# Last adjacency pair in two loads, one cast and some row ends moved between engines, and a later read of the flag that guards a second pass

## Chip, cores and metric

The kernel runs on one core of a Trainium2 chip. The metric is the device time of one execution in microseconds: the median of three runs is 112.62 us, with a lowest of 112.59 and a highest of 112.67.

## What is computed

Eight graphs of 1024 nodes with 128 features each. `adj` holds 0 or 1 as int32, so of the four relations only the first can occur, and the weights of the others matter only in a second pass described below.

```python
# x: (8, 1024, 128) f32, adj: (8, 1024, 1024) int32, weight: (4, 128, 128), bias: (128,)
masks = (relation[None] == rel_ids[:, None, None, None]).astype(x.dtype)
h = einsum('rbnm,bmd->rbnd', masks, x)
y = einsum('rbnd,rdo->bno', h, weight) + bias
out = layernorm(x + y, axis=-1)        # eps 1e-5, no gain and no offset
```

The adjacency is 33.6 MB of the 37.8 MB that are read; 4.2 MB are written.

## The kernel before, in words

A *unit* is 128 rows of the adjacency of one batch (512 KB, `adj_sb[:, slot, u]`), a *pair* two of them (1 MB), a *group* four units, or fewer in the last batch, which is split into a (units 0, 1), a2 (2, 3), c (4, 5), e (6) and d (7). `LAST` is the index of group a. A *set* of rows is what is normalised and stored together: one for each of the batches 0 to 6 (the seventh is called `full`), and two for batch 7, `ra` (units 0 to 3) and `rb` (units 4 to 7).

Loads. SyncE's queue issues all adjacency loads in order, batch 0 a unit at a time and the others a pair at a time (L414), with the loads of x between them; a slot of `adj_sb` is filled again when the pair that lay in it three batches before has been read by ScalarE (L408). After the last load the same queue issues the nine stores (L417), each when its set is normalised.

ScalarE reads each pair once, in `check` (L548): it writes `bytes_of` (fp8, two units interleaved, so that one transpose carries both) and leaves in `squares` a sum that is too large if an entry is neither 0 nor 1. It also copies `h` out of PSUM (L568), casts x to fp16 for batches 0 and 1 (L561), masks the last two odd units (L597), takes roots (L573) and normalises some rows (L583).

TensorE transposes a pair (L667) or, in batch 0, a unit (L658), multiplies the masked unit by the high and low part of x (L689), and projects with the weight (L702). For the last two batches x times the weight (`z`) is formed at the start and the product is direct (`rows_of_unit`, L743). `idle_turns` (L759) are matmuls of zeros ahead of the first unit. In `step_by_two` (L793) the transpose of the next pair stands before the two products of the group; for the pairs 4 and 5 alone it stands between them (L799 to L803).

VectorE masks the transposed unit (L875), adds x (L885), takes statistics (L891, L897, L902), the first guess of the inverse root (L912, `offer_guess`), and for `rb` the whole root (L917 to L936) and the rows of e and d (L941). `find_far` and `find` (L953 to L967) reduce what was gathered about the inputs to `found`; TensorE sums it (L838), VectorE copies the sum to `again` (L1048), and every engine loads `again` into a register and branches over a second pass (L301) that does not run on these inputs.

GpSimd casts x to fp16 for the batches from 2 on (L453), forms the low part (L459), adds the bias (L465), refines the roots of all sets but `rb` (L484 to L501) and normalises most rows (L512).

The end, in the order of the programs. GpSimd: roots of `full`, units 0 to 3 of `full`, roots of `ra`, units 0 and 1 of `ra`, unit 4 of `rb`. ScalarE: masks of units 5 and 7, root of `ra`, units 4 to 7 of `full`, root of `rb`, units 2 and 3 of `ra`, unit 5 of `rb`. VectorE: the list in the diff's last hunk. A store of one of the last three sets waits for GpSimd (`s_norm`) and for ScalarE (`s_aside`); that of `rb` for VectorE too (`s_done`). SyncE then branches at L301 and waits for the stores to land (L295, L296), which ends the program.

Of the kernel before, what the change touches and what calls it, by code (L numbers as in the profile page):

```python
# [5 lines left out]
P = 128  # L6
# [15 lines left out]
SLOPE = 4.25 ** 0.5  # L22
# [28 lines left out]
def adj_resnorm_kernel(nc, x, adj, weight, bias, out):  # L51
# [91 lines left out]
    with ctx:  # L143
# [49 lines left out]
        squares = sb("squares", [P, B * PAIRS], FP32)  # L193
# [40 lines left out]
        s_adj = [[sem(f"adj_loaded{slot}{k}") for k in range(PAIRS)] for slot in range(ADJ_SLOTS)]  # L234
        s_out = sem("rows_stored")
# [162 lines left out]
        def _(sp):  # L398
# [24 lines left out]
            load_x(1)  # L423
            for b in range(EARLY, B):
                for k in range(PAIRS):
                    load_adj(b, k)
                    if k == PAIRS - 1 and b + 1 < B - 2:
                        load_x(b + 1)
# [12 lines left out]
        def _(pool):  # L441
# [7 lines left out]
            def split_hi(b):  # L449
                pool.wait_ge(s_x[b], 16)  # L450
                pool.wait_ge(s_prod, last_group_of(b - 2) + 1)
                pool.wait_ge(s_rm, b - 1)
                nc.gpsimd.tensor_copy(x_hi[:, b % 2], x_sb[:, b]).then_inc(s_hi, 1)  # L453
# [66 lines left out]
            for b in range(B - 1):  # L520
                if b + 1 < B - 2:
                    if b:
                        split_hi(b + 1)
                    split_lo(b + 1)
                    add_bias(b + 1)
                if b >= 1:
                    roots(sets[b - 1])
                    normalise(sets[b - 1], sets[b - 1].units)
            full, ra, rb = sets[B - 2:]
            roots(full)  # L530
            normalise(full, full.units[:4])
# [6 lines left out]
        def _(act):  # L538
            def check(b, k):
# [5 lines left out]
                else:  # L545
# [4 lines left out]
                                     accum_out=squares[:, at:at + 1]).then_inc(s_check, 1)  # L550

# [64 lines left out]
            for g in groups[1:LAST]:  # L616
# [4 lines left out]
                for n, at in enumerate(range(pairs_checked_by(groups[g.index - 1]), pairs_checked_by(g))):  # L621
# [3 lines left out]
                    if n == 0 and g.index == 1:  # L625

                        split_hi(1, slice(0, J), s_x[1], s_hi)
# [3 lines left out]
            check(e.b, e.first // 2)  # L631
# [4 lines left out]
            normalise(full, full.units[4:]).then_inc(s_aside, 1)  # L636
            root(rb)
            normalise(ra, ra.units[2:]).then_inc(s_aside, 1)
# [4 lines left out]
        def _(pe):  # L643
# [119 lines left out]
            idle_turns(20, 2)  # L763
# [29 lines left out]
            def step_by_two(g, units, b, k):  # L793
                if not packed(b, k):
# [3 lines left out]
                    products(g, units, x_lo)  # L798
                elif pair_no(b, k) < FIRST_PACKED + 2:  # L799

                    products(g, units, x_hi)
                    transpose_pair(b, k)
                    products(g, units, x_lo)  # L803
                else:
                    transpose_pair(b, k)
                    for part in (x_hi, x_lo):
                        products(g, units, part)
# [35 lines left out]
        def _(dve):  # L843
            s_odd, s_far, s_wrong = (sem(n) for n in ("odd_ready", "far_ready", "wrong_ready"))
            s_st = sem("stats_ready")
# [113 lines left out]
            def find():  # L959

                dve.wait_ge(s_check, B * PAIRS)
                nc.vector.tensor_reduce(odd[:, 2:3], squares[:, :], AX.X, ALU.max).then_inc(s_odd, 1)
                dve.wait_ge(s_odd, 3)
                nc.vector.tensor_scalar(wrong[:, :], odd[:, 2:3], 2.0 * N * MIDDLE + 4.0, None, ALU.is_gt).then_inc(s_wrong, 1)
                dve.wait_ge(s_far, 2)
# [27 lines left out]
            for g in groups[1:LAST]:  # L993
# [9 lines left out]
                if g.index == LAST - 1:  # L1003
# [24 lines left out]
            statistics(a)  # L1028
            mask_unit(e.b, e.first)
            sum_rows(a2)  # L1030
            offer_guess(r)
            statistics(a2)
            combine(ra, a2, ra.units)
            sum_rows(c)
            statistics(c)
            combine(rb, c, c.units)
            offer_guess(ra)
            statistics_of_sum(e)
            combine(rb, e, e.units)
            statistics_of_sum(d)  # L1040
            combine(rb, d, d.units)
            find()
# [4 lines left out]
            dve.wait_ge(s_count, 1)  # L1047
            nc.vector.tensor_copy(again[:, :], ids_t[1][0:1, 0, 0:2].bitcast(FP32)).then_inc(s_again, 1)  # L1048
# [18 lines left out]
```

## Time and profile before

| | |
|---|---|
| median of three runs | 112.62 us |
| the profiled execution | 112.82 us |
| its span | 110.9 us |
| mean granted TensorE clock | 0.978 |
| busy | PE 89%, DVE 77%, ACT 76%, POOL 63% |
| DMA over the span | 42.23 MB, mean 381 GB/s |

The profile shows one execution on the core. The span is the stretch from its first to its last instruction, and 1.9 us of the profiled time lie outside of it. PE is TensorE's matmul side, PEld its weight loads, DVE VectorE, ACT ScalarE, POOL GpSimd, SP SyncE; a trailing q marks an engine's queue, where it issues transfers, waits or branches. L548 is line 548 of the kernel. All times in rows are microseconds from the start of the span unless ns is written.

### The profile page before, as it was taken

What the parts mean: (1) busy time and instruction counts of PE and PEld (TensorE: products, weight loads), DVE (VectorE), ACT (ScalarE), POOL (GpSimd) and SP (SyncE); (2) the same over time, 40 slices, a digit from 0 to 9 for tenths busy, and PEclk for the clock granted to TensorE, in tenths of its full rate; (3) what the DMA queues carried; (4) which work ended last, traced back from release to release, by engine and by line L of the source; (5) the groups of instructions that cost most, each with busy time, mean ns of one, the idle gap of its engine ahead of it and who ended that gap; (6) DMA issues with size and microseconds to landing.
All of it is one profiled execution on the core that took longest, in us unless ns stands there. A gap on an engine that the chain in (4) does not pass through costs nothing.

```text
span 110.9 us, 3073 instructions
## 1 busy us (share of the span) xinstructions
PE 99.1 (89%) x1118; PEld 91.6 (83%) x1118; DVE 85.2 (77%) x254; ACT 84.5 (76%) x103; POOL 70.1 (63%) x135
## 2 busy tenths in 40 slices
PE   5969999998999999999999999999999999996000
PEld 4639999997898999999998999899999999996000
DVE  1034677548999999999999896989794999999600
ACT  0444758999969897979798978996979998778320
POOL 3000699006969899989998999895187049518720
PEclk9999999999999999999999999999999999999965
DMA  3999999999999999999999999999999999991450
GB/s 50 359 420 420 421 422 440 419 425 422 420 425 425 422 428 417 425 427 420 427 422 424 427 425 422 428 428 428 414 425 428 419 424 418 408 384 74 191 191 9
DMA packets 7794, 42.23 MB, mean 381 GB/s; under 512 B 865, under 2 KB 994, under 8 KB 4194
## 3 DMA queue, kind: packets, MB, share of 16 engines
q1 hardware_dynamic: 7344, 40.44, 88.1%
q10 hardware_dynamic: 434, 1.57, 3.6%
q8 instruction: 10, 0.16, 0.6%
q14 instruction: 6, 0.05, 0.1%
HBM read 37.81 MB, written 4.19 MB: 379 GB/s over the span
## 4 chain that ended last, share of the span: by engine, by line
PE 52%; DMA 27%; ACT 6%; POOL 5%; DVE 2%; issue 2%; SPq 1%; POOLq 0%; DVEq 0%
DMA adj_sb<-adj 27%; PE h_ps L689 19%; PE h_ps L743 8%; PE ids_t L667 8%; ACT bytes_of L548 6%; PE y_ps L702 5%; PE ids_t L658 4%; POOL x_sb L512 3%; DVE mask_t L875 2%; PE y_ps L743 2%; SPq L414 1%; PE spare L722 1%; PE h_ps L722 1%; PE y_ps L722 1%; PE other L722 1%
## 5 line engine op out<-in xcount | busy, mean ns | idle before, releaser
L548 ACT ACTIVATE bytes_of<-adj_sb,offset 128x2048 fp8e4<-128x2048 int32 x32 | 64.0, 2003 | 4.3 <-DMA adj_sb<-adj 3.8
L875 DVE TENSOR_SCALAR mask_t<-ids_t 128x1024 uint16<-128x1024 uint16 x62 | 40.0, 681 | 11.8 <-PE ids_t L658 10.9
L689 PE MATMUL h_ps<-mask_t,x_hi 128*128 128x256 bf16 (+1 forms) x200 | 25.5, 272 | 0.9 <-DVE mask_t L875 0.9
L689 PE MATMUL h_ps<-mask_t,x_lo 128*128 128x256 bf16 (+1 forms) x200 | 25.5, 272 | 0.0
L512 POOL TENSOR_SCALAR x_sb<-x_sb,rstd,shift 128x128 f32<-128x128 f32 x55 | 23.8, 449 | 0.9
L689 PEld LDWEIGHTS h_ps<-mask_t,x_hi 128*128 128x128 f16 x200 | 18.3, 100 | 3.5 <-DVE mask_t L875 1.7
L465 POOL TENSOR_TENSOR x_sb<-x_sb,bias_sb 128x1024 f32<-128x1024 f32 x6 | 14.3, 2380 | 10.7 <-ACT bias_sb L609 10.3
L689 PEld LDWEIGHTS h_ps<-mask_t,x_lo 128*128 128x128 f16 x200 | 19.3, 100 | 2.1
L667 PE MATMUL ids_t<-ident,bytes_of 128*128 128x128 bf16 x224 | 18.6, 226 | 0.1
L667 PEld LDWEIGHTS ids_t<-ident,bytes_of 128*128 128x128 bf16 x224 | 17.2, 148 | 0.7 <-ACT bytes_of L548 0.5
L459 POOL TENSOR_TENSOR x_lo<-x_sb,x_hi 128x1024 f16<-128x1024 f32 x5 | 10.7, 2143 | 7.2 <-ACT x_hi L561 6.9
L891 DVE BATCH_NORM_STATS2 stats<-x_sb 128x6 f32<-128x128 f32 x62 | 13.6, 280 | 0.0
L702 PE MATMUL y_ps<-w_sb,h_all 128*128 128x128 f32 x96 | 12.7, 276 | 0.0
L568 ACT ACTIVATE h_all<-h_ps 128x512 f32<-128x512 f32 x12 | 7.2, 597 | 6.2 <-PE h_ps L689 6.2
L702 PEld LDWEIGHTS y_ps<-w_sb,h_all 128*128 128x128 f32 x96 | 11.7, 192 | 0.1
L743 PE MATMUL h_ps<-z_hi,mask_t 128*128 128x128 f16 x96 | 11.4, 220 | 0.0
L743 PE MATMUL h_ps<-z_lo,mask_t 128*128 128x128 f16 x96 | 11.4, 220 | 0.0
L885 DVE TENSOR_TENSOR x_sb<-y_ps,x_sb 128x512 f32<-128x512 f32 (+1 forms) x13 | 8.6, 663 | 3.4 <-PE y_ps L702 3.3
L743 PEld LDWEIGHTS h_ps<-z_hi,mask_t 128*128 128x128 bf16 x96 | 9.4, 98 | 0.0
L743 PEld LDWEIGHTS h_ps<-z_lo,mask_t 128*128 128x128 bf16 x96 | 9.4, 98 | 0.0
L850 DVE TENSOR_REDUCE row_max<-x_hi 128x8 f32<-128x1024 f16 x6 | 7.3, 1210 | 0.0
L759 PE MATMUL h_ps<-mask_t 128*128 128x256 bf16 (+1 forms) x22 | 5.5, 430 | 1.2 <-DVE mask_t L970 1.2
(102 smaller groups left out, 107.8 us busy)
## 6 DMA issues: line engine op xcount, KB each, us to landing
adj_sb<-adj SPq DMA_DIRECT2D x28, 1024.0 KB, 24.6
adj_sb<-adj SPq DMA_DIRECT2D x8, 512.0 KB, 10.1
out<-x_sb SPq DMA_DIRECT2D x7, 512.0 KB, 21.3
x_sb<-x SPq DMA_DIRECT2D x5, 512.0 KB, 24.1
x_sb<-x ACTq DMA_DIRECT2D x3, 512.0 KB, 7.5
out<-x_sb SPq DMA_DIRECT2D x2, 256.0 KB, 3.2
w_sb<-weight SPq DMA_DIRECT2D x1, 64.0 KB, 6.0
bias_row<-bias ACTq DMA_DIRECT2D x1, 0.5 KB
```

What stands on the lines that cost most here:

```text
L459: nc.gpsimd.tensor_tensor(x_lo[:, b % 2], x_sb[:, b], x_hi[:, b % 2], ALU.subtract).then_inc(s_lo, 1)
L465: nc.gpsimd.tensor_tensor(x_sb[:, b], x_sb[:, b], bias_sb[:, :].unsqueeze(1).to_broadcast([P, J, D]), ALU.add).then_inc(s_xb, 1)
L512: last = nc.gpsimd.tensor_scalar(rows[:, slot, u, :], rows[:, slot, u, :], rstd[:, slot, u:u + 1], shift[:, slot, u:u + 1], ALU.mult, ALU.add)
L548: nc.scalar.activation(bytes_of[:, at % ROOM].rearrange("p n t -> p t n"), adj_sb[:, slot, 2 * k:2 * k + 2, :], ACT.Square, scale=SLOPE, b ...
L667: last = nc.tensor.transpose(bank[:, j, :], words[:, j // step(b), j % step(b), :], ident[:, :])
L689: last = nc.tensor.matmul(h_ps[g.bank][:, to], part[:, g.b % 2, j, :], mask_t[:, g.b % 2, j, cols], start=(j == 0 and part is x_hi), stop= ...
L702: last = nc.tensor.matmul(y_of(g)[:, n, :], h_all[:, g.bank, n * P:(n + 1) * P], w_sb[:, 0, :], start=True, stop=True)
L743: last = nc.tensor.matmul(y_of(g)[:, u - g.first, :], mask_t[:, g.b % 2, j, u * P:(u + 1) * P], part[:, g.b - (B - 2), j, :], start=(j == ...
L850: nc.vector.tensor_reduce(row_max[:, b, :], x_hi[:, b % 2], AX.X, ALU.max, apply_absolute_value=True).then_inc(s_rm, 1)
L875: nc.vector.tensor_scalar(mask_t[:, b % 2, :, u * P:(u + 1) * P].bitcast(UINT16), ids_t[bank_of(turn)][:, :, :].bitcast(UINT16), 1 << bit, ...
L885: nc.vector.tensor_tensor(rows[:, g.b, g.us, :], y_of(g)[:, 0:g.count, :], x_sb[:, g.b, g.us, :], ALU.add).then_inc(s_sum, 1)
L891: last = nc.vector.bn_stats(stats[:, u, :], rows[:, g.b, u, :])
```

## The change

- The last pair (batch 7, units 6 and 7) is loaded as two units with a semaphore each; ScalarE reads them one by one into the same place of `bytes_of`, and their two sums are joined by a new VectorE instruction.
- The high part of x for batch 1 is cast by GpSimd and no longer by ScalarE.
- The transposes of pairs 4 and 5 stand before both products, as the others do.
- `idle_turns` at the start are 44 of 128 columns where there were 20 of 256.
- `find_far` comes one group earlier. `find` is cut into four: join, largest, wrong, and the rest, which are spread over the last groups and stand ahead of the combination for e.
- `offer_guess` of `full` stands ahead of the mask of e.
- Units 2 and 3 of `full` pass from GpSimd to ScalarE, which does them after the root of `rb`; the signal that lets `full` be stored is now theirs.
- VectorE copies `again` only when all rows have been normalised by GpSimd and ScalarE.

```diff
-        squares = sb("squares", [P, B * PAIRS], FP32)
+        squares = sb("squares", [P, B * PAIRS + 1], FP32)
...
+            def load_last(u, signal):
+                free(B - 1, u // 2)
+                sp.dma_start(adj_sb[:, (B - 1) % ADJ_SLOTS, u:u + 1, :], rows_of(adj, B - 1, u, 1)).then_inc(signal, 16)
+
             for b in range(EARLY, B):
                 for k in range(PAIRS):
+                    if (b, k) == (B - 1, PAIRS - 1):
+                        load_last(J - 2, s_first)
+                        load_last(J - 1, s_second)
+                        continue
                     load_adj(b, k)
...
                 if b + 1 < B - 2:
-                    if b:
-                        split_hi(b + 1)
+                    split_hi(b + 1)
                     split_lo(b + 1)
...
             roots(full)
-            normalise(full, full.units[:4])
+            normalise(full, full.units[:2])
             roots(ra)
...
+            def check_last_pair():
+                at = B * PAIRS - 1
+                room(at)
+                for t, loaded in enumerate((s_first, s_second)):
+                    act.wait_ge(loaded, 16)
+                    last = nc.scalar.activation(bytes_of[:, at % ROOM, :, t], adj_sb[:, (B - 1) % ADJ_SLOTS, J - 2 + t, :],
+                                                ACT.Square, scale=SLOPE, bias=offset[:, 0:1], saturate=False,
+                                                accum_out=squares[:, at + t:at + t + 1])
+                last.then_inc(s_check, 1)
...
-                    if n == 0 and g.index == 1:
-
-                        split_hi(1, slice(0, J), s_x[1], s_hi)
...
-            check(e.b, e.first // 2)
+            check_last_pair()
             root(full)
             mask_second(c.units[1])
             mask_second(d.first)
             root(ra)
-            normalise(full, full.units[4:]).then_inc(s_aside, 1)
+            normalise(full, full.units[4:])
             root(rb)
+            normalise(full, full.units[2:4]).then_inc(s_aside, 1)
             normalise(ra, ra.units[2:]).then_inc(s_aside, 1)
...
-            idle_turns(20, 2)
+            idle_turns(44, 1)
...
-                elif pair_no(b, k) < FIRST_PACKED + 2:
-
-                    products(g, units, x_hi)
-                    transpose_pair(b, k)
-                    products(g, units, x_lo)
                 else:
...
+            def join_last_pair():
                 dve.wait_ge(s_check, B * PAIRS)
-                nc.vector.tensor_reduce(odd[:, 2:3], squares[:, :], AX.X, ALU.max).then_inc(s_odd, 1)
+                last = B * PAIRS - 1
+                nc.vector.tensor_tensor(squares[:, last:last + 1], squares[:, last:last + 1], squares[:, last + 1:last + 2],
+                                        ALU.add).then_inc(s_joined, 1)
+
+            def find_largest():
+                dve.wait_ge(s_joined, 1)
+                nc.vector.tensor_reduce(odd[:, 2:3], squares[:, 0:B * PAIRS], AX.X, ALU.max).then_inc(s_odd, 1)
...
-                if g.index == LAST - 1:
+                if g.index == LAST - 2:
                     find_far()
...
             statistics(a)
+            offer_guess(r)
             mask_unit(e.b, e.first)
+            join_last_pair()
             sum_rows(a2)
-            offer_guess(r)
+            find_largest()
             statistics(a2)
             combine(ra, a2, ra.units)
             sum_rows(c)
+            find_wrong()
             statistics(c)
             combine(rb, c, c.units)
             offer_guess(ra)
             statistics_of_sum(e)
+            find()
             combine(rb, e, e.units)
             statistics_of_sum(d)
             combine(rb, d, d.units)
-            find()
...
             dve.wait_ge(s_count, 1)
+
+            dve.wait_ge(s_norm, len(sets))
+            dve.wait_ge(s_aside, 3)
             nc.vector.tensor_copy(again[:, :], ids_t[1][0:1, 0, 0:2].bitcast(FP32)).then_inc(s_again, 1)
```

## Rows read from the trace of the kernel before

**Rows 1.** The page's 40 equal slices of the span: DMA engines' busy share, in tenths.
```profile
DMA  3999999999999999999999999999999999991450
```

**Rows 2.** The chain that ended last: start us, us, what.
```profile
44.68 24.71 DMA adj_sb<-adj
...
71.57 0.71 PE ids_t L667 x8
...
97.69 0.51 PE ids_t L667 x8
```

**Rows 3.** Timeline of the first 28 us: start, us, engine, line, instruction, count, [idle before].
```profile
1.19 4.45 PE L759 MATMUL h_ps<-mask_t 128*128 128x256 bf16 x20 [1.19 <-DVE mask_t L970]
...
24.91 1.07 ACT L561 ACTIVATE x_hi<-x_sb 128x1024 f16<-128x1024 f32 x1
...
27.89 1.05 PE L689 MATMUL h_ps<-mask_t,x_hi 128*128 128x256 bf16 x8 [0.51 <-DVE mask_t L875]
```

**Rows 4.** Timeline of ScalarE: its pass over the last pair.
```profile
93.88 2.01 ACT L548 ACTIVATE bytes_of<-adj_sb,offset 128x2048 fp8e4<-128x2048 int32 x1 [0.29 <-DMA adj_sb<-adj]
```

**Rows 5.** Timeline of VectorE, 98 to 105 us.
```profile
98.22 0.69 DVE L875 TENSOR_SCALAR mask_t<-ids_t 128x1024 uint16<-128x1024 uint16 x1 [0.21 <-PE ids_t L667]
...
99.16 0.20 DVE L912 RECIPROCAL first_guess<-std 128x8 f32<-128x8 f32 x1
...
101.57 0.18 DVE L902 BATCH_NORM_AGGREGATE moments<-stats 128x2 f32<-128x6 f32 x1
101.80 0.30 DVE L897 BATCH_NORM_STATS2 stats<-spare 128x6 f32<-128x128 f32 x1
102.13 0.18 DVE L902 BATCH_NORM_AGGREGATE moments<-stats 128x2 f32<-128x6 f32 x1
102.23 0.15 DVE L962 TENSOR_REDUCE odd<-squares 128x1 f32<-128x32 f32 x1
...
103.03 0.27 DVE L967 TENSOR_SCALAR found<-wrong,high,low 128x1 f32<-128x1 f32 x1 [0.46 <-DVE wrong L964]
...
104.73 0.13 DVE L1048 CAST again<-ids_t 1x1 int32<-1x1 f32 x1
```

**Rows 6.** Timeline of GpSimd and ScalarE, 99 to 106 us.
```profile
99.51 0.20 POOL L489 TENSOR_TENSOR product<-sixteenth,first_guess 128x8 f32<-128x8 f32 x1 [2.19 <-DVE first_guess L912]
...
100.99 1.74 POOL L512 TENSOR_SCALAR x_sb<-x_sb,rstd,shift 128x128 f32<-128x128 f32 x4
...
102.46 0.28 ACT L573 ACTIVATE std<-moments,eps 128x4 f32<-128x4 f32 x1
...
104.68 1.26 ACT L583 ACTIVATE x_sb<-x_sb,shift,rstd 128x128 f32<-128x128 f32 x3 [1.94 <-POOL shift L501]
104.76 1.31 POOL L512 TENSOR_SCALAR x_sb<-x_sb,rstd,shift 128x128 f32<-128x128 f32 x3
```

**Rows 7.** Timeline of SyncE's queue: the stores of `full` and of `rb`.
```profile
102.75 0.33 SPq L417 DMA_DIRECT2D out<-x_sb  x1
```
```profile
106.10 0.37 SPq L417 DMA_DIRECT2D out<-x_sb  x1
```

**Rows 8.** Stretches: length, PE, PEld, DVE, ACT, POOL busy (count), PEclk, DMA share, GB/s.
```profile
103.50:104.75 1.25, 0.05 (x2) 0.00 (x0) 1.15 (x7) 0.07 (x1) 0.83 (x4) 1.00 0.96 390
...
106.50:107.75 1.25, 0.00 (x0) 0.00 (x0) 0.00 (x0) 0.00 (x0) 0.00 (x0) 0.50 1.09 405
...
108.50:110.00 1.50, 0.00 (x0) 0.00 (x0) 0.00 (x0) 0.00 (x0) 0.00 (x0) 0.50 0.07 16
```

**Rows 9.** DMA begun in 107.4:107.7: packets, MB, share of 16 engines over 0.3 us.
```profile
q8 instruction: 1, 0.02, 28.7%
```

**Rows 10.** DMA issues from 106 us on: count, KB, us from issue to landing.
```profile
out<-x_sb SPq DMA_DIRECT2D x1, 256.0 KB, 4.3
```

**Rows 11.** Queue instructions of two lines: count, ns min/median/max, first and last start.
```profile
L301 PEldq COMPARE_BRANCH  x1: 453/453/453, 105.8 to 105.8; - x1
```
```profile
L296 SPq EVENT_SEMAPHORE  x1: 17/17/17, 110.4 to 110.4; - x1
```

More of the change, by code:

```diff
@@ L234, in adj_resnorm_kernel @@
         s_adj = [[sem(f"adj_loaded{slot}{k}") for k in range(PAIRS)] for slot in range(ADJ_SLOTS)]
+        s_first, s_second = sem("last_pair_first_unit_loaded"), sem("last_pair_second_unit_loaded")
         s_out = sem("rows_stored")
@@ L450, in split_hi @@
                 pool.wait_ge(s_x[b], 16)
-                pool.wait_ge(s_prod, last_group_of(b - 2) + 1)
-                pool.wait_ge(s_rm, b - 1)
+                if b >= 2:
+                    pool.wait_ge(s_prod, last_group_of(b - 2) + 1)
+                    pool.wait_ge(s_rm, b - 1)
                 nc.gpsimd.tensor_copy(x_hi[:, b % 2], x_sb[:, b]).then_inc(s_hi, 1)
@@ L844, in _ @@
             s_odd, s_far, s_wrong = (sem(n) for n in ("odd_ready", "far_ready", "wrong_ready"))
+            s_joined = sem("last_squares_joined")
             s_st = sem("stats_ready")
@@ L957, in find_far, with find_wrong, find @@
                 nc.vector.tensor_scalar(low[:, :], odd[:, 1:2], LEAST, None, ALU.is_lt).then_inc(s_far, 1)
-            def find():
+            def join_last_pair():
                 dve.wait_ge(s_check, B * PAIRS)
-                nc.vector.tensor_reduce(odd[:, 2:3], squares[:, :], AX.X, ALU.max).then_inc(s_odd, 1)
+                last = B * PAIRS - 1
[4 more added lines that the diff above has]
+                nc.vector.tensor_reduce(odd[:, 2:3], squares[:, 0:B * PAIRS], AX.X, ALU.max).then_inc(s_odd, 1)
+            def find_wrong():
                 dve.wait_ge(s_odd, 3)
                 nc.vector.tensor_scalar(wrong[:, :], odd[:, 2:3], 2.0 * N * MIDDLE + 4.0, None, ALU.is_gt).then_inc(s_wrong, 1)
+            def find():
                 dve.wait_ge(s_far, 2)
```

## The prediction

> **What bounds the kernel now.** I read the page's slices first, then the chain of work that ended last, then the timeline of every engine over the last 15 us, and last the DMA traffic after the final store. The slices show the DMA engines full from the second slice to the thirty-sixth [rows 1]: the loads never pause. The chain shows what that means for the front of the kernel. It goes back from TensorE's transposes at 71.57 through ScalarE's pass over a pair to a load that was issued at 44.68 and landed 24.71 us later, at 69.39 [rows 2]. So up to 71.57 the time is set by how fast bytes arrive, and TensorE, though almost always busy, is there only as early as the data. From 71.57 to the transposes of the last pair at 97.69 the chain is TensorE's own work in one piece [rows 2]. Then comes an end that belongs to the small engines and the stores: the last matmul is over about 101.75 (VectorE's statistics of the last unit start at 101.80 [rows 5]), the last store is issued at 106.10 [rows 7], lands 4.3 us later [rows 10], SyncE passes its last wait at 110.4 [rows 11], and the span ends at 110.9. Nine microseconds therefore lie behind the last product. That is where I look for an effect.
>
> **The front: idle turns, cast, transposes.** The 20 turns of 256 columns take 4.45 us, 0.22 each [rows 3]; 44 of 128 columns at half that pace take 4.9 and end near 6.1, still before or at the first unit, whose transposes start at 6.37 in the chain's time. The cast of 1.07 us leaves ScalarE at 24.91 [rows 3] and goes to GpSimd, which has a hole there. The moved transposes fill a stall of TensorE of 0.51 us at 27.89, where it waits for a mask [rows 3]; VectorE's own order is not changed there, so the mask itself comes at most 0.1 to 0.2 us sooner. Between 0 and 0.7 us is won at 28 us. What hides it is the load that lands at 69.39: TensorE would only wait longer at 71.57 [rows 2]. I cost all three at nothing, and keep 0.3 us of gain as the outer bound, in case a part passes the load.
>
> **The last pair in two loads.** ScalarE starts on the pair at 93.88, 0.29 us after it was free, and takes 2.01 [rows 4], so `bytes_of` is there at about 95.9; TensorE comes for it just before 97.69 [rows 2]. In two halves the first can start earlier and the second ends, at a 1024-column price of 1.07 each [rows 3], by 95.7 to 96.1. Gain and loss both lie under 1.6 us of cover. They would count only if the second unit landed more than 1.6 us late. Nothing.
>
> **VectorE's end.** `find_far` moves into a gap. The first guess of `full` is now taken before the mask at 98.22, ahead of which VectorE idles 0.21 us [rows 5], so at about 97.95 in place of 99.16: 1.2 us earlier. Against that, three small instructions (join, largest, wrong) and the last of `find` now come before the statistics of d. A small one costs about 0.10, the distance of 102.13 to 102.23 [rows 5]; `found` 0.2 to 0.3. Less the guess that left (0.12) this is 0.3 to 0.4 us, with only 0.05 of slack (101.57 + 0.18 against 101.80 [rows 5]). So the variances of `rb` come 0.3 later and its root on ScalarE at 102.8, not 102.46 [rows 6]. It is paid back at once: before, `found` stood in front of the inversion and began at 103.03 after 0.46 us of idling [rows 5], so the inversion started at 103.2; now nothing stands there and it starts at 103.1. At worst `found` idles 0.46 in its new place too, and everything of `rb` comes 0.4 later.
>
> **GpSimd and ScalarE.** GpSimd takes 1.48 us from the first product to the first row (99.51 to 100.99) and 0.43 a row [rows 6]. With the guess 1.2 earlier it starts on `full` at 99.8 and is through its two rows at 100.7, not 102.7. The roots of `ra` then wait for VectorE's guess of `ra`, which follows the combination of c and comes some 0.2 before the 101.57 of e's, so by 101.4, and give rows from 103.2 on, not 104.76 [rows 6]; GpSimd ends at 104.6. ScalarE does `full` 4 to 7 from 100.5 to 102.2, the root of `rb` at 102.8, and then five rows in one go. Three took 1.26, so 0.39 a row and 0.49 for the last [rows 6]: from 103.0, `full` is complete at 103.9, `ra` at 104.65, `rb` at 105.05. ScalarE is now last. The store of `full` is issued at 103.9, 1.15 later than the 102.75 of before; that of `rb` at 105.05, 1.05 earlier than 106.10 [rows 7].
>
> **The stores.** Bytes of `full` flow from 103.5, 0.8 us after its issue, for 1.3 us; those of `ra` and `rb`, together as many, from 106.5 for another 1.3 to 1.4 [rows 8]. Now they queue behind one another: 103.9 + 0.8 + 2.65 = 107.35, against 107.9. If only this counted, the gain would be 0.5 us, not 1.05.
>
> **The wait before `again`.** This is the step that decides. After 107.9 the DMA engines are almost still, yet SyncE waits to 110.4. What moves in between is a trickle of 16 GB/s, some 24 KB between 108.5 and 110.0 [rows 8]: packets of the last store on one engine. That engine had been given something else. At about 107.5 a packet of the instruction queue begins, 16 KB, with 28.7% of 16 engines times 0.3 us, that is 1.38 us on a single engine [rows 9]. I take it to be caused by the branch over the second pass: `again` is there at 104.86 [rows 5], TensorE's branch runs at 105.8 and takes 453 ns [rows 11], and the fetch begins 2.65 us after `again`. Before, it fell into the middle of the last store's bytes. Now VectorE holds `again` for ScalarE's last row. Queued behind that wait are only the copy and VectorE's own branch; who waits for the copy is the branch of each engine, SyncE's among them, and that comes after the stores are issued and needs 1 us, long before they land. `again` comes at 105.05 + 0.1 to 0.5 (the 0.46 of `found` is the nearest row for a VectorE instruction after a late second wait) + 0.13 = 105.3 to 105.7, and the fetch at 107.9 to 108.3, when the bytes have been gone since 107.35. The last store then lands, like before, 0.5 us after its last byte (110.4 against 109.9), at 107.85, and the span ends 0.5 us after that (110.9 against 110.4), at 108.4.
>
> The Trainium skill has a rule on this (Runtime: NRT & Kernel Launch, Instruction fetch mechanics): engines stream their instructions in blocks of 16 KiB through DMA, which is "mostly hidden", and a taken branch to a place outside the window forces a fetch before the engine goes on. The size agrees with the packet in the row; "mostly hidden" does not, since here the fetch seems to hold up a store. By the word hidden the wait would be worth nothing.
>
> **The sum.** Span 110.9 to 108.4, less 2.5 us. Of the profiled 112.82 that leaves 110.3; the median lies 0.2 below the profiled execution, so 112.62 - 2.5 = 110.1. I add 0.1 for the worse end of `found`: 110.2.
>
> **Rivals.**
> 1. *A part of the collision stays* (0.20). A smaller instruction fetch falls among the 2.65 us of queued bytes, or the fetches come earlier than reckoned. It costs the engine 0.5 to 1.4 us of the 2.5: 110.7 to 111.6. For it: the queue of bytes is now longer. Against it: 0.55 us of margin.
> 2. *The fetch is not the cause* (0.11): the trickle belongs to an engine that is behind anyway. Then only the stores' 0.5 us remain, 112.1. Against it: the trickle follows right on the fetch [rows 8, 9].
> 3. *Slower* (0.10). `full` is stored 1.15 later, and the bytes of all three sets end late on the one engine. If they end after 107.9, the fetch still meets them, but starts later than before: what followed its start at 107.5 took 2.9 us to the landing, so 107.9 to 108.3 + 2.9 = 110.8 to 111.2, a span of 111.3 to 111.7 and 113.0 to 113.4 us. It decides from 0.55 us of lateness on.
> 4. *The front's gain passes the loads* (0.06), on top of my forecast: 109.9. Rows 2 speak against it.
> 5. *Gains and losses of the end cancel* (0.03), at 112.6.
>
> **How the numbers follow.** My forecast has 0.50, at 109.9 to 110.6 by the bounds of `found` and of the copy. With rivals 1, 2 and 4 the chance of faster is 0.87, of no change 0.03, of slower 0.10. About 0.2% is what a measurement of this kernel can tell from no change. The range goes from 109.8 to 112.1, which leaves out rivals 3 and 5 and some of the edges.
>
> **What would show it.** Right: the idle of 0.51 at 28 us gone and a longer wait for ScalarE or the load near 71; TensorE's last transposes still near 97.7; `full` stored near 103.9 and `rb` near 105.1; the copy of `again` after 105.1; the 16 KB instruction packet after the last store's bytes; a landing of 2.8 us in place of 4.3. Wrong: the last transposes earlier than 97.4 (then the loads didn't hold the front), or a last landing still over 4 us.

## The result and the profile after

The changed kernel takes 109.77 us (median of four runs, 109.71 to 109.82), where the one before takes 112.65 beside it. The ratio is 0.974, with a 95% interval of 0.9722 to 0.9757: 2.9 us less. The forecast was 110.2, with a range that began at 109.8. So the direction holds and the mechanism of the wait too, the gain was put 0.4 us too small, and the time lies 0.03 us below the range of 109.8 to 112.1. The profiled execution has a span of 107.9 us.

The chain that ended last, after (start us, us, what; the load's number of L414 is L416 here, L667 is L686):

```profile
44.71 24.71 DMA adj_sb<-adj
...
71.60 0.71 PE ids_t L686 x8
...
97.72 0.51 PE ids_t L686 x8
```

These are [rows 2] moved by 0.03 us. The front of the kernel has changed and everything from the load at 44.71 on stands where it stood. Nothing of the front's changes is to be seen at 71.60. ScalarE's pass over the last pair (timeline of ScalarE) comes in two parts of 1.14 us, at 93.52 and 94.65, that end at 95.8, 1.9 us before TensorE wants them. The second is:

```profile
94.65 1.14 ACT L568 ACTIVATE bytes_of<-adj_sb,offset 128x1024 fp8e4<-128x1024 int32 x1
```

All of the gain is made behind 97.6 us. First VectorE's timeline there, the answer to [rows 5]:

```profile
97.64 0.19 DVE L927 RECIPROCAL first_guess<-std 128x8 f32<-128x8 f32 x1
98.25 0.69 DVE L890 TENSOR_SCALAR mask_t<-ids_t 128x1024 uint16<-128x1024 uint16 x1 [0.43 <-PE ids_t L686]
98.86 0.15 DVE L978 TENSOR_TENSOR squares<-squares 128x1 f32<-128x1 f32 x1
...
99.38 0.49 DVE L906 BATCH_NORM_STATS2 stats<-x_sb 128x6 f32<-128x128 f32 x2
...
100.20 0.39 DVE L900 TENSOR_TENSOR x_sb<-h_ps,x_sb 128x256 f32<-128x256 f32 x1
100.50 0.14 DVE L987 TENSOR_SCALAR wrong<-odd 128x1 f32<-128x1 f32 x1
100.62 0.49 DVE L906 BATCH_NORM_STATS2 stats<-x_sb 128x6 f32<-128x128 f32 x2
...
101.37 0.27 DVE L912 BATCH_NORM_STATS2 stats<-other 128x6 f32<-128x128 f32 x1
101.55 0.26 DVE L992 TENSOR_SCALAR found<-wrong,high,low 128x1 f32<-128x1 f32 x1
101.73 0.17 DVE L917 BATCH_NORM_AGGREGATE moments<-stats 128x2 f32<-128x6 f32 x1
101.83 0.30 DVE L912 BATCH_NORM_STATS2 stats<-spare 128x6 f32<-128x128 f32 x1
102.16 0.18 DVE L917 BATCH_NORM_AGGREGATE moments<-stats 128x2 f32<-128x6 f32 x1
102.71 0.18 DVE L932 RECIPROCAL last_guess<-std 128x4 f32<-128x4 f32 x1 [0.36 <-ACT std L594]
...
104.73 0.15 DVE L1079 CAST again<-ids_t 1x1 int32<-1x1 f32 x1 [0.35 <-ACT x_sb L604]
```

The guess of `full` is at 97.64 in place of 99.16. The last combination, at 102.16, is 0.03 us later than before, although join, largest, wrong and found now stand ahead of it. The inversion starts at 102.71; before, it had to let `found` pass and started at 103.2. Two more rows of before, the statistics of a2 and of e, are compared with 99.38 and 101.37 further down:

```profile
99.28 0.49 DVE L891 BATCH_NORM_STATS2 stats<-x_sb 128x6 f32<-128x128 f32 x2
...
101.27 0.27 DVE L897 BATCH_NORM_STATS2 stats<-other 128x6 f32<-128x128 f32 x1
```

GpSimd and ScalarE (their timelines, the answer to [rows 6]):

```profile
97.98 0.20 POOL L500 TENSOR_TENSOR product<-sixteenth,first_guess 128x8 f32<-128x8 f32 x1 [0.94 <-DVE first_guess L927]
...
99.47 0.89 POOL L523 TENSOR_SCALAR x_sb<-x_sb,rstd,shift 128x128 f32<-128x128 f32 x2
...
103.07 1.33 POOL L523 TENSOR_SCALAR x_sb<-x_sb,rstd,shift 128x128 f32<-128x128 f32 x3
```
```profile
102.58 2.02 ACT L604 ACTIVATE x_sb<-x_sb,shift,rstd 128x128 f32<-128x128 f32 x5
```

The last row is ready at 104.60 on ScalarE, and at 106.07 before. The stores follow (SyncE's timeline, then the window 106 to 107 and the one behind it, with the columns of [rows 8]):

```profile
103.52 1.10 SPq L419 DMA_DIRECT2D out<-x_sb  x2
104.72 0.40 SPq L419 DMA_DIRECT2D out<-x_sb  x1
```
```profile
106.00:107.00 1.00, 0.00 (x0) 0.00 (x0) 0.00 (x0) 0.00 (x0) 0.00 (x0) 0.50 0.97 371
107.00:107.50 0.50, 0.00 (x0) 0.00 (x0) 0.00 (x0) 0.00 (x0) 0.00 (x0) 0.50 0.07 16
```

The bytes of all three sets flow without a gap until 107.0 and stop; no trickle follows. The instruction packets come after them. This is the DMA traffic of the window 107.3 to 107.7, in 40 slices of 0.01 us, where the only two slices with bytes are the starts of an 8 KB packet at 107.46 and of a 16 KB one at 107.63:

```profile
GB/s 0 0 0 0 0 0 0 0 0 0 0 0 0 0 0 0 819 0 0 0 0 0 0 0 0 0 0 0 0 0 0 0 0 1638 0 0 0 0 0 0
...
q8 instruction: 1, 0.02, 17.6%
```

SyncE passes its last wait at 107.4, before: 110.4 [rows 11] (the wait's line, L298 here):

```profile
L298 SPq EVENT_SEMAPHORE  x1: 17/17/17, 107.4 to 107.4; - x1
```

### The profile page after: what moved, and what is told of

Read it like the earlier page. It is cut to its first block, busy times and chain, and to the rows that moved or that the text cites. A ratio compares the mean times of both kernels' runs of the same rounds, so it can differ in the third digit from the quotient of the medians.

```text
span 107.9 us, 3126 instructions
## 1 busy us (share of the span) xinstructions
PE 99.2 (92%) x1142; PEld 92.2 (85%) x1142; DVE 85.0 (79%) x255; ACT 85.4 (79%) x106; POOL 70.5 (65%) x134
## 4 chain that ended last, share of the span: by engine, by line
DMA 45%; PE 25%; SPq 16%; ACT 6%; DVE 3%; issue 2%; DVEq 0%
DMA adj_sb<-adj 45%; SPq L416 10%; PE h_ps L762 8%; PE h_ps L708 6%; PE ids_t L686 5%; ACT bytes_of L558 4%; SPq L405 3%; PE y_ps L721 3%; ACT x_sb L604 2%; PE y_ps L762 2%; SPq L402 1%; DVE stats L906 1%; DVE moments L917 1%; DVE x_sb L900 1%; SPq L394 0%
## 5 line engine op out<-in xcount | busy, mean ns | idle before, releaser
L558 ACT ACTIVATE bytes_of<-adj_sb,offset 128x2048 fp8e4<-128x2048 int32 x31 | 62.1, 2003 | 5.9 <-DMA adj_sb<-adj 5.3
L523 POOL TENSOR_SCALAR x_sb<-x_sb,rstd,shift 128x128 f32<-128x128 f32 x53 | 23.1, 456 | 0.9
L686 PE MATMUL ids_t<-ident,bytes_of 128*128 128x128 bf16 x224 | 19.0, 228 | 0.5 <-ACT bytes_of L558 0.5
L686 PEld LDWEIGHTS ids_t<-ident,bytes_of 128*128 128x128 bf16 x224 | 16.9, 148 | 2.4 <-ACT bytes_of L558 2.1
L721 PE MATMUL y_ps<-w_sb,h_all 128*128 128x128 f32 x96 | 12.7, 276 | 0.0
L470 POOL TENSOR_TENSOR x_lo<-x_sb,x_hi 128x1024 f16<-128x1024 f32 x5 | 10.7, 2140 | 0.4
L464 POOL CAST x_hi<-x_sb 128x1024 f16<-128x1024 f32 x5 | 5.2, 1047 | 6.7 <-DMA x_sb<-x 6.7
```

What stands on the lines that cost most here:

```text
L470: nc.gpsimd.tensor_tensor(x_lo[:, b % 2], x_sb[:, b], x_hi[:, b % 2], ALU.subtract).then_inc(s_lo, 1)
L523: last = nc.gpsimd.tensor_scalar(rows[:, slot, u, :], rows[:, slot, u, :], rstd[:, slot, u:u + 1], shift[:, slot, u:u + 1], ALU.mult, ALU.add)
L558: nc.scalar.activation(bytes_of[:, at % ROOM].rearrange("p n t -> p t n"), adj_sb[:, slot, 2 * k:2 * k + 2, :], ACT.Square, scale=SLOPE, b ...
L686: last = nc.tensor.transpose(bank[:, j, :], words[:, j // step(b), j % step(b), :], ident[:, :])
L721: last = nc.tensor.matmul(y_of(g)[:, n, :], h_all[:, g.bank, n * P:(n + 1) * P], w_sb[:, 0, :], start=True, stop=True)
```

## Experiments

The moment at which TensorE is done with the last pair shifts from execution to execution by a few tenths, with the landing of the load that holds the front. So beside each span stands the start of VectorE's mask for unit 6 (the row with `mask_t<-ids_t` at 98.25 above), which follows TensorE's last transposes at once, and the *end*, the span less that start. It is the end that the changes behind 97.6 us act on. Span, mask and end are those of one profiled execution of each kernel; the medians are of 4 executions (9 for `a_early`), and each ratio is to executions of the kernel before that ran beside them, with medians of 112.41 us (`a_early` to `a_nofront`), 112.44 (`a_rows4`, `a_find_late`) and 112.61 (the last four). Spans are given to 0.1.

| kernel | median us | ratio to before, 95% interval | span | mask of unit 6 | end |
|---|---|---|---|---|---|
| before | 112.65 | | 110.9 | 98.22 | 12.7 |
| changed | 109.77 | 0.974 (0.9722 to 0.9757) | 107.9 | 98.25 | 9.7 |
| a_early | 111.81 | 0.9937 (0.9907 to 0.9967) | 110.2 | 98.62 | 11.6 |
| a_nowait | 109.91 | 0.9769 (0.9719 to 0.9819) | 108.1 | 98.40 | 9.7 |
| b_wait | 110.90 | 0.988 (0.98 to 0.9959) | 109.0 | 98.37 | 10.6 |
| a_nofront | 109.56 | 0.9743 (0.9695 to 0.9792) | 107.6 | 97.92 | 9.7 |
| a_rows4 | 109.02 | 0.9686 (0.9654 to 0.9717) | 107.2 | 98.11 | 9.1 |
| a_find_late | 109.89 | 0.9773 (0.9743 to 0.9802) | 107.9 | 98.20 | 9.7 |
| r4_guess_late | 110.76 | 0.9837 (0.9796 to 0.9877) | 109.1 | 98.39 | 10.7 |
| r4_find_late | 109.37 | 0.9703 (0.9658 to 0.9749) | 107.7 | 98.52 | 9.2 |
| r4_oneload | 109.09 | 0.9709 (0.9664 to 0.9753) | 107.2 | 98.10 | 9.1 |
| r4_nowait | 109.12 | 0.9696 (0.9658 to 0.9734) | 107.3 | 98.24 | 9.1 |

### Does the flag's fetch hold up the stores?

The theory says that the copy of `again` sets off a 16 KB instruction fetch some 2.6 us later, which costs if bytes of the last store are still queued on its DMA engine. The rival says that the trickle of [rows 8] belongs to an engine that is slow anyway. `b_wait` adds only the wait to the kernel before:

```diff
             dve.wait_ge(s_count, 1)
+            dve.wait_ge(s_norm, len(sets))
+            dve.wait_ge(s_aside, 3)
             nc.vector.tensor_copy(again[:, :], ...)
```

> The kernel before, with nothing but the two waits ahead of the flag's copy. Theory of the fetch: the copy comes at 106.2 to 106.5, the 16 KB fetch at 108.9, a microsecond after the last bytes (107.9); the last store lands at 108.4, the span ends at 108.9 and not 110.9, time 110.6. So the wait alone would be worth 2.0 of the 2.9 us. Rival (slow engine): span 110.9 or slightly more, since the branches come later; time 112.6.

Measured: span 109.0, end 10.6 for 12.7, median 110.90 where the kernel before beside it has 112.41. The copy is at 106.31, the bytes are through by 108.0, and SyncE's wait is over at 108.5 (rows of the windows and of the wait's line, L296; the two instruction packets start at 108.7 to 108.9):

```profile
107.00:108.00 1.00, 0.00 (x0) 0.00 (x0) 0.00 (x0) 0.00 (x0) 0.00 (x0) 0.50 0.99 381
108.00:108.60 0.60, 0.00 (x0) 0.00 (x0) 0.00 (x0) 0.00 (x0) 0.00 (x0) 0.50 0.02 3
```
```profile
L296 SPq EVENT_SEMAPHORE  x1: 17/17/17, 108.5 to 108.5; - x1
```

The rows are stored at the same moments as before, counted from the mask of unit 6, and the trickle is gone. A wait that makes the flag 1.6 us later ends the kernel 2.1 us earlier by the two profiled executions. By the medians it is 1.5 us, and the interval of the ratio reaches from 0.5 to 2.2 us.

A part of the difference, and what the trickle is, can be read from the DMA traffic of the kernel before, in 40 slices of the windows 107.4:107.7 and 108.7:110.3:

```profile
GB/s 1092 273 546 0 0 273 273 546 0 546 1092 546 819 0 0 1 2458 546 273 273 546 1365 273 546 0 0 0 273 819 0 546 546 1092 273 546 0 0 273 273 546
```
```profile
GB/s 0 0 0 0 51 0 0 0 0 0 51 0 0 0 0 51 0 0 0 51 0 51 0 51 0 51 0 51 0 0 0 0 0 0 0 0 0 0 0 0
```

The 16 KB packet starts in the slice with 2458, at 107.52, and with the 1.38 us of [rows 9] it ends at 108.90; the first packet of the trickle starts in the slice from 108.86 to 108.90. So the trickle is what the engine with the fetch had left to do. The 1 just ahead of the fetch is the packet of 4 bytes with which an engine closes its part of a transfer, here of the store of `ra`. The other fifteen of them lie in 107.1 to 107.3. The engine was therefore about 0.2 us behind when the fetch came, and the rival has this much of the trickle on its side; why it was behind is open. `a_early` goes the other way in the changed kernel:

```diff
+            dve.wait_ge(s_count, 1)
+            nc.vector.tensor_copy(again[:, :], ...).then_inc(s_again, 1)
             for part in (invert, times_guess, times_guess_again, better_guess, shift_last):
...
-            dve.wait_ge(s_count, 1)
-            dve.wait_ge(s_norm, len(sets))
-            dve.wait_ge(s_aside, 3)
-            nc.vector.tensor_copy(again[:, :], ...).then_inc(s_again, 1)
```

> The changed kernel, but VectorE copies the flag right after the combination for d, without waiting for any row. Theory (the instruction fetches that follow the flag hold up the last stores): the 16 KB fetch follows the copy by 2.6 to 2.8 us, so it begins at 105.0 to 105.3, in the middle of the bytes of the last three stores (104.2 to 107.05 in the changed kernel). It costs their engine 1.1 to 1.7 us: span 109.0 to 109.7 instead of 107.9, time 110.9 to 111.5. Rival (the trickle at the end belongs to a slow engine, the flag has no part in it): span 107.9, or less because the last branches are over sooner; time 109.7 to 109.8.

Measured: span 110.2, end 11.6 for 9.7. The fetch lies where it was expected, in the window 104.80 to 104.95, among the bytes, and 62.3% of 16 engines times 0.15 us is 1.5 us of one engine (rows: that packet; the store of `rb`; all nine stores' issues, with their shortest, median and longest time in ns; the end of SyncE's last wait):

```profile
q8 instruction: 1, 0.02, 62.3%
```
```profile
105.09 1.58 SPq L419 DMA_DIRECT2D out<-x_sb  x1
```
```profile
L419 SPq DMA_DIRECT2D out<-x_sb x9: 332/1584/2106, 73.3 to 105.1; - x9
```
```profile
L298 SPq EVENT_SEMAPHORE  x1: 17/17/17, 109.6 to 109.6; - x1
```

The loss of 1.9 us is above the 1.1 to 1.7 that I gave it. The second row offers a reason: the issue of the last store takes 1.58 us in place of 0.40, and ends at 106.67, 0.3 us after the fetch. That the fetch holds it is argued and not shown, since the four issues of stores from 73 to 80 us, under the full traffic of the loads, take 2.10 us each in this run as in the changed kernel.

The two runs move nothing but the flag. The trickle goes when the flag is later and comes back when it is earlier (in `a_early` one engine still moves bytes at 109.19, the others are done by 107.96), which an engine that is slow by itself would not do. They don't part TensorE's 16 KB packet from whatever else follows the flag; but of the two instruction packets that come behind the flag it is the only one that starts before the other engines' last bytes, in the kernel before and in `a_early` alike; the one of 8 KB starts at 108.56 and 108.65, when they are done. From the start of the copy to that of this packet it is 2.2 to 2.9 us over these runs (102.63 to 104.87, 104.73 to 107.63). `a_nowait` takes the waits alone away and leaves the copy behind the rows of d:

```diff
             dve.wait_ge(s_count, 1)
-            dve.wait_ge(s_norm, len(sets))
-            dve.wait_ge(s_aside, 3)
             nc.vector.tensor_copy(again[:, :], ...)
```

> The changed kernel without the two waits ahead of the flag's copy; the copy still stands after the rows of d, so it comes at about 104.3 and not 104.73. Theory of the fetch: its start moves from 107.5 to about 107.0, just at the end of the last bytes at 107.04: between nothing and 1.4 us, span 107.9 to 109.3, most likely 108.2. Rival: 107.9 exactly, as the bytes end at the same time. With the early copy beside it this gives the dose: the farther ahead of the last bytes the flag comes, the longer the end.

Measured: end 9.7, as with the waits. The copy is at 104.44, and in the window 107.0 to 107.4 the trace has the last bytes and the start of the 16 KB packet (19.5% of 16 engines times 0.4 us, 1.25 us):

```profile
q8 instruction: 1, 0.02, 19.5%
```

It is a near miss: the last closing packet is at 107.19, and the fetch begins at 107.21. So in the changed kernel the waits are an insurance and not the gain itself. What moved the bytes ahead of the fetch there is that the rows are done 1.5 us earlier, while the copy, without its waits, would be only about 0.5 us earlier than before, counted from the mask of unit 6 (104.44 with the mask at 98.40, for 104.73 with the mask at 98.22). In the kernel before, the waits alone do it.

### Does the front count?

`a_nofront` puts the front of before into the changed kernel:

```diff
-            idle_turns(44, 1)
+            idle_turns(20, 2)
...
+                elif pair_no(b, k) < FIRST_PACKED + 2:
+                    products(g, units, x_hi)
+                    transpose_pair(b, k)
+                    products(g, units, x_lo)
...
-                    split_hi(b + 1)
+                    if b:
+                        split_hi(b + 1)
...
+                    if n == 0 and g.index == 1:
+                        split_hi(1, slice(0, J), s_x[1], s_hi)
```

> The changed kernel with the front as before: 20 idle turns of 256 columns, the transposes of pairs 4 and 5 between the products, the cast for batch 1 on ScalarE. Theory (the load that lands at 69.4 holds the front): transposes after it at 71.6 and the last ones at 97.7 as in both kernels, span 107.9 within 0.1, time 109.8. Rival (a part of the gain is the front's): 0.3 to 0.7 us longer, 110.1 to 110.5.

Measured: ratio 0.9743, the same as with the new front, and the same end. That the gain is absorbed by the loads, and not by VectorE, was to be shown by two kernels (one execution each) that load half as much from batch 3 on. Their output isn't the reference's, since half of each row is left over from an earlier batch.

```diff
+                cols = slice(0, N // 2 if b >= ADJ_SLOTS else N)
-                sp.dma_start(units_of(adj_sb[:, slot], b, 2 * k, 2), rows_of(adj, b, 2 * k, 2)).then_inc(s_adj[slot][k], 16)
+                sp.dma_start(units_of(adj_sb[:, slot], b, 2 * k, 2)[:, :, cols],
+                             rows_of(adj, b, 2 * k, 2)[:, :, cols]).then_inc(s_adj[slot][k], 16)
```

> The changed kernel, but from batch 3 on only the first half of each row of the adjacency is loaded (the last pair excepted); the rest is what an earlier batch left there, so 10 MB less come in and the output differs. Theory (the loads absorb the front's gain): no wait for a load between 45 and 94 us; with the loads out of the way TensorE's lead at 35 us is kept to the end, so that the last transposes come 0.4 to 0.9 us earlier than in the same kernel with the old front, its twin in this call.

> The twin: the old front (idle turns, transposes, cast) with the same halved loads from batch 3 on. Theory: last transposes 0.4 to 0.9 us later than with the new front. Rival (VectorE, which has hardly a gap between 28 and 58 us, gives the pace and takes the gain): no difference over 0.2 us, and the loads need not be named.

The pair gives the rival's answer. Its two executions differ by 0.07 us at 35 us, and by 0.07 at 72 us and at the end; the expected 0.4 to 0.9 was wrong. VectorE's masks near 35 and near 72 us, in the order before, changed, h_front, h_nofront:

```profile
35.23 1.25 DVE L875 TENSOR_SCALAR mask_t<-ids_t 128x1024 uint16<-128x1024 uint16 x2
...
72.32 0.69 DVE L875 TENSOR_SCALAR mask_t<-ids_t 128x1024 uint16<-128x1024 uint16 x1 [0.34 <-PE ids_t L667]
```
```profile
34.33 1.26 DVE L890 TENSOR_SCALAR mask_t<-ids_t 128x1024 uint16<-128x1024 uint16 x2
...
72.34 0.69 DVE L890 TENSOR_SCALAR mask_t<-ids_t 128x1024 uint16<-128x1024 uint16 x1 [0.35 <-PE ids_t L686]
```
```profile
35.13 1.26 DVE L891 TENSOR_SCALAR mask_t<-ids_t 128x1024 uint16<-128x1024 uint16 x2
...
71.76 1.29 DVE L891 TENSOR_SCALAR mask_t<-ids_t 128x1024 uint16<-128x1024 uint16 x2
```
```profile
35.20 1.26 DVE L899 TENSOR_SCALAR mask_t<-ids_t 128x1024 uint16<-128x1024 uint16 x2
...
71.83 1.29 DVE L899 TENSOR_SCALAR mask_t<-ids_t 128x1024 uint16<-128x1024 uint16 x2
```

With half the bytes the way from the first to the second takes 36.63 us in both. With all of them it takes 37.09 before and 38.01 in the changed kernel, which is 0.90 us ahead of the kernel before at 35 and level at 72. So the loads do take back a lead, and VectorE, which can do this way in 36.63, does not.

But the lead of 0.90 us is not the front's. Two more kernels with the old front and all loads have the same mask at 34.55 (`b_wait`) and 34.42 (`a_nofront`); the nine with the new front and all loads have it at 34.33 to 34.74. It is the profiled execution of before, at 35.23, that is late. The row of `a_nofront`, and VectorE in the 7 us before, in the changed kernel (the columns of [rows 8]):

```profile
34.42 1.26 DVE L898 TENSOR_SCALAR mask_t<-ids_t 128x1024 uint16<-128x1024 uint16 x2
```
```profile
28.00:35.00 7.00, 7.00 (x74) 6.49 (x72) 6.97 (x21) 5.86 (x6) 3.51 (x3) 1.00 1.02 430
```

TensorE's stall of 0.51 us near 28 us is gone with the new front (in `a_nofront` it is there, at 27.10), and nothing of it is left at 35. VectorE is busy for 6.97 of the 7 us between, 6.96 before, which fits the rival: it gives the pace there. That it is the cause is not shown. What these executions show is no gain above 0.1 us at 35 us, so the loads had nothing of the front to hide.

### What are the moves at the end worth?

`a_rows4` gives `full` its four rows on GpSimd back:

```diff
-            normalise(full, full.units[:2])
+            normalise(full, full.units[:4])
...
-            normalise(full, full.units[4:])
+            normalise(full, full.units[4:]).then_inc(s_aside, 1)
             root(rb)
-            normalise(full, full.units[2:4]).then_inc(s_aside, 1)
```

> The changed kernel with one part undone: GpSimd normalises units 0 to 3 of the set of batch 6 again, ScalarE units 4 to 7 only, so this set may be stored at about 102.2 and not 103.5. Theory (the 1 MB of the last three sets queues on the DMA engines and ends 2.7 us after the first bytes, whatever row is last): the first half is gone before the second begins, the last rows are ready at 104.6 to 104.7 as before, the last bytes go at 106.1 and not 107.05, span 107.0, time 108.8 to 109.0. Rival (the last row sets the end): span 107.9 to 108.1, since GpSimd has two rows more and the roots of the next set come 0.1 to 0.2 later.

Measured: 109.02 us, end 9.1 for 9.7. This version is faster than both kernels. GpSimd has time for the two rows while it waits for the guess of `ra` (idle 0.65 us there in the changed kernel). The store of `full` is issued at 102.08, 1.4 us earlier, and its bytes are gone before the others begin (SyncE's timeline and the windows):

```profile
102.08 0.33 SPq L419 DMA_DIRECT2D out<-x_sb  x1
...
104.04 0.81 SPq L419 DMA_DIRECT2D out<-x_sb  x2
```
```profile
104.25:104.75 0.50, 0.00 (x0) 0.00 (x0) 0.14 (x1) 0.05 (x1) 0.19 (x1) 0.81 0.00 0
104.75:106.25 1.50, 0.00 (x0) 0.00 (x0) 0.00 (x0) 0.00 (x0) 0.00 (x0) 0.50 0.91 350
```

So the move of the two rows, one part of the change, costs 0.6 us. The runs whose names begin with r4 start from this version. `r4_guess_late` moves the guess back:

```diff
-            offer_guess(r)
             mask_unit(e.b, e.first)
             join_last_pair()
             sum_rows(a2)
+            offer_guess(r)
             find_largest()
```

> The version with four rows of batch 6 on GpSimd (span 107.2, 109.0 us), with the first guess of that set back behind the sum of a2 (99.2 and not 97.6). Theory (the early guess is what makes GpSimd's end short, as it does two sets of roots and seven rows in one line): its first row at 100.8 and not 99.3, the roots of the next set at 104.4 and not 103.0, GpSimd's last row at 105.8 and not 104.4, so the last bytes go 1.3 us later: span 108.4 to 108.6, 110.3 us. Rival (the queue of bytes hides it, as in the changed kernel): span under 107.6.

Measured: span 109.1, end 10.7 for 9.1. GpSimd's four rows start at 101.22 and its last ones at 104.99 (its timeline):

```profile
101.22 1.74 POOL L523 TENSOR_SCALAR x_sb<-x_sb,rstd,shift 128x128 f32<-128x128 f32 x4
...
104.99 1.31 POOL L523 TENSOR_SCALAR x_sb<-x_sb,rstd,shift 128x128 f32<-128x128 f32 x3
```

One instruction of 0.19 us, moved by 1.5 us, is worth 1.6 us (1.7 by the ratios). The search was put back in both versions:

```diff
-            join_last_pair()
...
-            find_largest()
...
-            find_wrong()
...
-            find()
             combine(rb, e, e.units)
             statistics_of_sum(d)
             combine(rb, d, d.units)
+            join_last_pair()
+            find_largest()
+            find_wrong()
+            find()
```

> The changed kernel with join, largest, wrong and the rest in one piece behind the combination for d, where the search stood before. Theory (the small instructions cost nothing where they are now, because VectorE waits for TensorE there, and cost 0.7 to 1.1 us ahead of the inversion): rstd of the last set comes at 104.0 to 104.4 and not 103.3, the last rows at 105.0 to 105.3; the bytes queue, so the end moves by 0 to 0.5 us: span 107.9 to 108.4. Rival (they are also hidden at the end, behind ScalarE's root): span 107.9, rstd 0.3 later at most.

> The same version with the search in one piece behind the combination for d. It puts rstd of the last set 0.4 us later, as seen (103.7 for 103.3). Theory (with the stores no longer in one queue of bytes, the last row counts again): last row on VectorE at 104.7, last store 0.2 to 0.3 us later, span 107.4 to 107.5, 109.3 us. Rival: nothing, as GpSimd is last and not VectorE; span 107.2.

Measured: ends of 9.7 for 9.7, and 9.2 for 9.1. The root of `rb` does come later, but by 0.3 to 0.4 us and not by the 0.7 to 1.1 expected: in `a_find_late` the last combination starts at 102.11 and the inversion at 103.04 behind `found`, not at 102.71. This is close to the rival's figure.

```profile
103.04 0.17 DVE L932 RECIPROCAL last_guess<-std 128x4 f32<-128x4 f32 x1
```

In `a_find_late` ScalarE's five rows, which end at 104.57, and the queue of bytes cover this. In `r4_find_late` the last store is issued 0.3 us later, counted from the mask, and the end grows by less than 0.1, where 0.2 to 0.3 was expected. The search is worth 0 to 0.1 us. Last, the pair in one load, and the waits once more:

```diff
-                    if (b, k) == (B - 1, PAIRS - 1):
-                        load_last(J - 2, s_first)
-                        load_last(J - 1, s_second)
-                        continue
...
-            check_last_pair()
+            check(e.b, e.first // 2)
...
-                dve.wait_ge(s_joined, 1)
+                dve.wait_ge(s_check, B * PAIRS)
...
-            join_last_pair()
```

> The same version with the last pair in one load and one pass of ScalarE, without the joining instruction. Theory (1.6 us of cover between ScalarE's end and TensorE's transposes): no change, span 107.2 within 0.2. Rival (the second unit's earlier end is worth something): 0.2 to 0.4 us longer.

```diff
-            dve.wait_ge(s_norm, len(sets))
-            dve.wait_ge(s_aside, 3)
```

> The same version without the two waits ahead of the flag's copy. The copy comes at 104.25, so the 16 KB fetch at 106.8 to 106.9, and the last bytes go at 106.3. Theory (only a fetch that begins before the last bytes costs): no change, span 107.2 within 0.2. Rival (the waits help in some other way, by keeping the other engines' branches off the stores): 0.5 us or more longer.

Measured: both 9.1, no change. Without the waits the 16 KB packet starts in the window 106.4 to 106.7, in the 25th of 40 slices, at 106.58; the last closing packets, the 1s at the start of the row, are over by 106.45:

```profile
GB/s 0 1 0 1 0 0 1 0 0 0 0 0 0 0 0 0 0 0 0 0 0 0 0 0 2185 0 0 0 0 0 0 0 0 0 0 0 0 0 0 0
```

## What the prediction had right, and the step that failed

- *The front, nothing:* right in the number, but not for the reason that I gave. The transposes at 71.6 and 97.7 did not move, and the old front in the new kernel gives the same time. The stall of 0.51 us was closed, but I put the gain of it between 0 and 0.7 us at 28 us and let the load hide it; at 35 us no more than 0.1 us of it is to be seen, with all loads or with half of them.
- *The last pair in two loads, nothing:* right, with 1.9 us of cover for the 1.6 that I gave; `r4_oneload` confirms it.
- *VectorE's end:* this is the step that failed. I charged three small instructions at 0.10 each, the distance between two independent ones, and `found` at 0.2 to 0.3, less 0.12 for the guess that left, against 0.05 of slack: 0.3 to 0.4 us. It was 0.03, and the mask of unit 6 is 0.03 later too. The rows say where the difference lies, each counted from that mask. Join and `largest`, less the guess, cost 0.07 (statistics of a2 at 99.38 for 99.28), as charged. `wrong` costs nothing: the statistics of c read the sum that the instruction before wrote (100.20 to 100.62), `wrong` starts at 100.50 while that sum is not yet through, and the statistics of e are still 0.07 late (101.37 for 101.27). `found` costs 0.06 and not 0.2 to 0.3 (the combination of e at 101.73 for 101.57), for the same reason. That makes 0.13 in place of 0.38 to 0.48. The slack was 0.13 and not 0.05: I counted a combination's whole 0.18, where the next instruction starts 0.10 after it (102.13 to 102.23 [rows 5]). The variances of `rb` came at 102.34 and not at 102.6.
- *ScalarE and GpSimd:* the guess came 1.5 us earlier, not 1.2. ScalarE's five rows take 2.02 us as reckoned (2.05), but start at 102.58 and not at 103.0. That is the same error passed on: `full` is complete at 103.5 (forecast 103.9), `rb` at 104.6 (105.05).
- *The stores:* right in kind. I said that the bytes would queue and that only 0.5 us would be left of an earlier last row. They do queue, and end at 107.0 (107.35). What I did not draw from my own number is that the later store of `full` made the queue; `a_rows4` puts this at 0.6 us lost.
- *The wait before `again`:* right in mechanism, wrong in whom it credits. In the kernel before, the waits are worth 1.5 us by the medians and 2.1 by the profiled executions (`b_wait`; I reckoned about 2). In the changed one they are worth nothing that these runs can tell (`a_nowait`), because without them the fetch starts just as the bytes end. The 16 KB fetch came at 107.63 and not at 107.9 to 108.3, since the flag came earlier with the rows; its margin to the last bytes was 0.6 us, that of the 8 KB one 0.4.
- *The sum:* 2.5 us of span were forecast, 3.0 measured: 107.9 for 108.4. VectorE's term put the store of `full` 0.4 us too late (103.9 for 103.52), and with it the last bytes by 0.3; the rest is the landing, 0.4 us after the last byte and not 0.5, and roundings. I had also added 0.1 us for a worse end of `found`, which put the forecast at 110.2. The low end of the range allowed 0.3 us beyond the sum, for the front; it should also have allowed for the small instructions being almost free.
- *Rivals:* that the fetch is not the cause is refuted by `b_wait` and `a_early`; about 0.2 us of lag on that engine is left to this rival. The collision that stays, and the one that makes the kernel slower, did not happen, but `a_early` shows that an early flag costs 1.9 us.

From the ends, of one profiled execution each, the change is: 12.7, less 2.1 for the bytes and the fetch kept apart, less 1.5 for the early guess and the search, plus 0.6 for the two rows on ScalarE, is 9.7. The middle term is what is left between `b_wait` (10.6) and `a_rows4` (9.1); `r4_guess_late` gives the guess nearly all of it. By the ratios of the table the same three terms are about 1.4, 2.2 and 0.6 us, so how the gain divides between the first two is known to some 0.7 us only.

The rule of the Trainium skill that I set against this step (Runtime: NRT & Kernel Launch, Instruction fetch mechanics) calls the cost of crossing a block mostly hidden. By that rule the wait would be worth nothing, and in the middle of the kernel no row here speaks against it. At the end it is not hidden: taking the two apart is worth 1.5 to 2.1 us (`b_wait`). The same section's remark that a taken branch may force a fetch fits what the traces show, with a packet of 16 KB about 1.1 to 1.7 us after TensorE's branch.

## What to carry to other kernels

Read what the DMA engines do after the last store is issued, and whose packets they are: a store that lands late may be waiting behind an instruction fetch that a branch in the epilogue has set off, and a few tenths between that fetch and the last bytes decided over 1.5 to 2 us here: it cost this much when it began 0.4 us before the other engines' last bytes, and nothing when it began 0.02 us after them. When several stores leave so close together that their bytes queue, the queue and not the last row sets the end, and the first bytes should start as soon as any set can be complete. A small independent instruction on VectorE in a chain of dependent ones cost 0 to 0.07 us here; price it by the gap it goes into, and not by the pace of a full engine. And before a lead in one trace is credited to a change, look for it in the other runs: the scatter between executions, 0.8 us at 35 us, was nearly as large as the lead.

## What was not expected of the hardware

- The issue of the last store took 1.58 us when a fetch ran beside it, and 0.40 in the changed kernel (`a_early`); that the fetch is the reason is not shown.
- A 16 KB instruction packet occupied its engine for 1.1 to 1.5 us at the end of these three kernels (17.6% of 16 engines times 0.4 us in the changed kernel, 1.38 us before, 1.5 in `a_early`).
- Making one engine wait longer shortened the whole kernel by 1.5 to 2.1 us without changing when any row was ready (`b_wait`).
